# Another order of TensorE's and VectorE's work in the first small attention of a Perceiver block

## What is computed

```python
q = (layernorm(x) @ q_w.T + q_b)           # 16 heads of 32
k, v = ctx @ k_w.T + k_b, ctx @ v_w.T + v_b
q, k = apply_rope(q) * 32 ** -0.5, apply_rope(k)
scores = einsum('bhqd,bhkd->bhqk', q, k)   # only keys k <= q (a window of 64, 64 queries)
probs = softmax(scores)
x = x + einsum('bhqk,bhkd->bhqd', probs, v) @ o_w.T + o_b
```

## Time and profile before

| | us |
|---|---|
| median of 3 runs | 1521.74 |
| lowest and highest | 1520.28 and 1524.32 |
| the profiled execution | 1517.1 |
| its span, first to last instruction | 1515.1 |
| its mean granted TensorE clock | 0.963 |
| TensorE busy in the span | 1413.3 (93%) |
| VectorE busy | 727.6 (48%) |
| ScalarE busy | 509.7 (34%) |

### The profile page before, as it was taken

One profiled execution on the slowest core, in us unless ns is written; L12 is line 12 of the kernel. 1 busy time (PEld: TensorE's weight loads), 2 busy tenths in 40 slices (PEclk: granted clock), 3 DMA queues, 4 the chain that ended last, 5 costly groups with the idle time before them and its releaser, 6 DMA issues. The chain is left out here.

```text
span 1515.1 us, 26710 instructions
## 1 busy us (share of the span) xinstructions
PE 1413.3 (93%) x11200; PEld 1054.6 (70%) x11200; DVE 727.6 (48%) x1337; ACT 509.7 (34%) x839; POOL 368.6 (24%) x228
## 2 busy tenths in 40 slices
PE   7879988899989999999999999999999997997995
PEld 6747765455447788888787888888878865434783
DVE  6659769798463323323322233223232233676833
ACT  3414322333121153333432534334325343613702
POOL 7111000000140422222332313122313111306911
PEclk9799969999989999999999999999999999999997
DMA  5403100102024121111110211111102016003000
GB/s 204 167 1 132 42 35 1 77 0 84 0 91 143 57 63 33 52 38 57 37 55 30 64 33 52 38 57 39 55 28 64 23 51 256 1 0 132 0 1 28
DMA packets 49573, 88.01 MB, mean 58 GB/s; under 512 B 28584, under 2 KB 41136, under 8 KB 46128
## 3 DMA queue, kind: packets, MB, share of 16 engines
q1 hardware_dynamic: 49456, 86.32, 16.4%
HBM read 76.61 MB, written 9.70 MB: 57 GB/s over the span
## 5 line engine op out<-in xcount | busy, mean ns | idle before, releaser
L1338 POOL TENSOR_TENSOR ctx_hi<-ctx_raw,one 128x1536 fp32r<-128x1536 f32 (+1 forms) x32 | 91.5, 2860 | 567.3 <-DMA ctx_raw<-in_ctx 347.0
L1536 ACT COPY ET<-PS 128x512 f32<-128x512 f32 (+1 forms) x224 | 129.5, 585 | 277.0 <-PE PS L1440 201.6
L1639 DVE TENSOR_SCALAR_CACHE_REDUCE E<-PS 128x384 f32<-128x384 f32 (+1 forms) x256 | 131.8, 571 | 180.6 <-PE PS L1417 180.1
L1608 DVE TENSOR_TENSOR V<-PS,vbias 128x512 f32<-128x512 f32 (+1 forms) x104 | 71.8, 691 | 193.0 <-PE PS L1384 192.8
L1384 PE MATMUL PS<-ctx_raw_r,wk_hi 128*128 128x384 f32 (+1 forms) x512 | 128.2, 355 | 0.0
L1384 PE MATMUL PS<-wv_lo,ctx_hi 128*128 128x512 f32 (+1 forms) x416 | 127.6, 406 | 0.0
L1543 ACT ACTIVATE E<-E,peak 128x1601 f32<-128x1601 f32 x64 | 103.5, 1622 | 66.9 <-DVE peak L1644 66.9
L1440 PE MATMUL PS<-ident,E 128*128 128x128 f32 (+1 forms) x832 | 122.9, 273 | 0.0
L1384 PE MATMUL PS<-ctx_hi,wk_hi 128*128 128x384 f32 (+1 forms) x512 | 120.6, 357 | 1.5 <-POOL ctx_raw_r L1341 1.5
L1384 PE MATMUL PS<-wv_hi,ctx_hi 128*128 128x512 f32 (+1 forms) x416 | 120.4, 411 | 0.8 <-issue 0.8
L1341 POOL TENSOR_TENSOR ctx_raw_r<-ctx_raw,ctx_hi 128x1536 fp32r<-128x1536 f32 (+1 forms) x32 | 116.9, 3654 | 2.5
(11 more groups left out here) (320 smaller groups left out, 2217.0 us busy)
## 6 DMA issues: line engine op xcount, KB each, us to landing
ctx_raw<-in_ctx SPq DMA_DIRECT2D x24, 768.0 KB, 4.4
ctx_raw<-in_ctx_first SPq DMA_DIRECT2D x8, 900.0 KB, 4.5
rel_scr<-rel_out SPq DMA_DIRECT2D x8, 640.0 KB, 3.6
fwk<-in_fwk SPq DMA_DIRECT2D x1, 4096.0 KB, 12.2
fwv<-in_fwv SPq DMA_DIRECT2D x1, 4096.0 KB, 12.5
corr<-rel_scr SPq DMA_DIRECT2D x64, 48.0 KB
p_scr<-E SPq DMA_DIRECT2D x16, 192.0 KB, 2.3
near<-p_scr SPq DMA_DIRECT2D x64, 48.0 KB
```

Of the source, the lines that this page charges most:

```text
L1338: nc.gpsimd.tensor_tensor(ctx_hi[r][:, :, 0:n], ctx_raw[r][:, :, 0:n], one[:].unsqueeze(1).broadcast_to([P, KC, n]), ALU.mult).then_inc(S[ ...
L1536: nc.scalar.copy(ET[0:n, j % ET_RING, :], src[0:n, :]).then_inc(S["et_out"], 1)
L1608: v.tensor_tensor(V[0:rows, at % V_RING, :], bank(4 + NUMBER[unit] % 2)[0:rows, :], vbias[0:rows, :], ALU.add).then_inc(S["v_out"], 1)
L1639: v.tensor_scalar(E[:, p, k0:k0 + n], bank(r)[:, 0:n], 1.0, None, ALU.mult, ALU.max, accum_out=tops[:, p, c:c + 1]).then_inc(S["s_out"], 1)
```

## The change

In the call with the mask TensorE's list becomes S0 S1 V0 S2 C0 V1 S3 C1 V2 P0 C2 V3 P1 C3 P2 P3. On VectorE the residuals and moments of tiles 0 to 2 no longer stand between the softening and weighting of the tiles but behind the last weighting. The waits inside each step stay as they are. The call without the mask keeps its order.

```diff
             pe.wait_ge(s.loaded[w_out], 16)
-            scores(0)
-            for t in range(NT):
-                if t + 1 < NT:
-                    scores(t + 1)
-                if t >= 1:
-                    project(t - 1)
-                values(t)
-                context(t)
-            project(NT - 1)
+            if mask:
+                scores(0), scores(1), values(0), scores(2), context(0), values(1), scores(3), context(1)
+                values(2), project(0), context(2), values(3), project(1), context(3), project(2), project(3)
+            else:
+                scores(0)
+                for t in range(NT):
+                    if t + 1 < NT:
+                        scores(t + 1)
+                    if t >= 1:
+                        project(t - 1)
+                    values(t)
+                    context(t)
+                project(NT - 1)
...
                 other(2)
-                if t >= 1:
+                if t >= 1 and not mask:
                     residual(t - 1)
             if beside:
                 beside.finish(dve, ch)
+            if mask:
+                for t in range(NT - 1):
+                    residual(t)
```

## The result

The changed kernel takes 1510.94 us (median of 4 runs, 1510.06 to 1514.17), the kernel before 1523.03 in the same comparison (1520.28 to 1524.35): a ratio of 0.9926, 95% interval 0.9907 to 0.9944. That is 8.5 to 14.2 us less, a clear gain of 0.6 to 0.9%. The forecast was 1517.4, 4.3 us less, with 0.54 on no change and 0.42 on faster.

What follows compares the result with a forecast made beforehand. TensorE, with idle holes and a low clock, was taken to bound the first small attention. Reordering gains 3.40 us, taken as 4.3 for an earlier clock rise: 1521.7 - 4.3 = 1517.4 us, range 1511.5 to 1521.5.

Steps and rivals of the forecast that it cites:

- The holes ahead of C, P and C: First small attention, TensorE: idle times ahead of contexts and projections, 8.89 us in all, the first 3.80.
- the six waits: TensorE's idle times in the first small attention; no wait was to replace them from scores of tile 2 on.
- rival A: First small attention: clock back before tile 3's scores, VectorE becomes the bound; gain 8.2 us, 1513.5; chance 0.12.
- That reading of the transposes: Start of next stage: only transposes at 0.50 from 113.90 to 116.50, clock 1.00 from 117.40; transposes bring it back.
- The forecast case: First small attention: clock rises inside tile 0's projection, 3 us in, projection 5.0 us; gain 2.2 to 5.7, chance 0.62.
- The tail: Stage's end: residuals and three applies on VectorE ready just as tile 3's projection ends; costed at nothing.
- Rival B: First small attention: clock stays low through the run of projections; 10.2 us slower, 1531.9; chance 0.04.
- Rival C: Later stages: one clock fall more, gain 1.1, 1520.6, chance 0.13; one fewer, gain 7.5, 1514.2, chance 0.08.
- The base: Whole kernel: forecast starts from the runs' median 1521.74, 4.6 above the profiled execution's 1517.1.

Runs made afterwards that it cites:

- short kernels: Kernel before and changed kernel, each cut off behind the first small attention with the state stored there: 121.71 us before, 112.11 after.
- second trace of after: Changed kernel run again without an edit for another trace, against the kernel before: 1510.86 us in 6 runs, ratio 0.9924.
- short_after: Changed kernel cut off behind the first small attention, state stored there: 112.11 us (6 runs) against 121.71 for the kernel before cut alike.
- short_s3_first: Against short_after, the scores of tile 3 moved ahead of the context of tile 0 and weight transposes of tile 1: 119.22 us (4 runs).
- before_again: Kernel before, unedited, run again for a second trace: 1521.64 us (12 runs), ratio 1.0003; its time in the trace comparison is 1520.87.
- first trace of after: First profiled execution of the changed kernel, no further edit: 1511.36 us; the changed kernel's median was 1510.94.
- projections_late_only: Against the kernel before, projections and residuals late as in the change, scores still one tile ahead behind the context: 1521.8 us (12 runs), ratio 1.0003.
- short_before: Kernel before cut off behind the first small attention, state stored there: 121.71 us (6 runs, 120.33 to 123.43).
- short_filled_six: Against short_after, six useless matmul products added in TensorE's holes of the first attention: 112.77 us (4 runs) against 112.11.

## Why the prediction was right or wrong

**The direction and the mechanism** were right. The holes ahead of C, P and C were the gain, S2 moved into the first of them with its mask addition ready (the sum has 0.89 us to spare, not over 0.9; in the first trace it was 0.2, 66.84 to 67.08). From S3 on nothing replaced the six waits in the first trace; in the second, two of A's did, 1.11 and 0.91 us. That this stage can give nearly the whole gain is shown by the short kernels (9.6 of some 10 us).

**The size was too small by more than half**, through one step: where the clock comes back. The forecast put it under P0 and so charged S3, C1 and V2 at the low clock, 3.26, 0.55 and 0.93 us more than now. In the second trace of after and in short_after the clock is back ahead of S3: S3 takes 3.71 and 3.68 us, C1 0.99 and V2 1.09, and VectorE becomes the bound. That was rival A, with a chance of 0.12. In the short runs five of six are as fast as the trace with A's picture. The argument against A was the uninterrupted S2 at 0.50, and it stands for scores: short_s3_first shows 14 us of them that don't bring the clock back. But it was applied to the wrong stretch. Between S2 and S3 stand C0 and V1, and the prediction itself read, from the transposes of the next stage, that transposes bring the clock back; it used this for P0 behind V2 and not for S3 behind V1. In no trace of before does a V follow a C without a hole between them in the low stretch, so the rows bounded this case only from afar; in hindsight 0.12 was too little.

**That reading of the transposes** is right for the trace that it was made from and doesn't hold in the next ones. The same 16 transposes start the next stage in the other three traces of the whole kernels, and there the clock came back only at 121.0 (before_again), 114.9 (first trace of after) and 113.8 (second), each time under later matmuls. The first line below is the second trace of after over these transposes. A longer run of them does bear the reading out: the feed-forward layer starts with transposes alone, and in all four traces the clock comes back under them. The other two lines are the first trace of after, where they start at 265.39.

```profile
104.60:108.10 3.50, 3.50 (x16) 3.14 (x16) 2.74 (x5) 2.77 (x5) 3.50 (x1) 0.50 0.77 248
265.50:268.40 2.90, 2.90 (x14) 2.54 (x15) 2.69 (x7) 1.27 (x3) 0.00 (x0) 0.50 0.76 233
269.40:273.50 4.10, 3.92 (x26) 2.52 (x24) 2.44 (x4) 2.46 (x5) 0.00 (x0) 1.00 1.01 434
```

**A's own working** was right step for step. Its start times against the second trace of after: S3 76.68 and 76.19, V2 81.3 and 80.81, P0 82.3 and 81.74, C2 87.1 and 86.45, P1 89.9 and 89.28, P2 94.3 and 93.73. The constant 0.5 to 0.6 is a term of its own: the slot of V at the low clock was taken as 1.97 us from a V0 with nothing behind it; with S2 behind it the slot is 66.10 - 64.34 = 1.76, twice. So A gives 8.2 + 0.4, and 8.9 was measured.

**The forecast case** came in the first trace from S3 on only: P0 4.95 us against 5.0, rise 2.8 us in against 3. Ahead of S3 the clock was low from S0 on, back for S2 (67.08, 3.74 us) and fell once more before S3. The prediction had one fall and one rise, at the places of before.

**The tail** cost nothing, as worked out. The last apply of tile 2 ends at 103.37, when P3 (96.01 + 7.13 = 103.14) has just ended, and residual(3) follows at once (103.28); it starts 3.8 us behind P3's start (99.5), 3.81 before.

```profile
102.82 0.55 DVE L97 TENSOR_SCALAR XN<-X,mean_var,rstd 128x512 f32<-128x512 f32 x1 [0.46 <-POOL rstd L112]
103.28 0.68 DVE L420 TENSOR_TENSOR X<-PS,X 128x512 f32<-128x512 f32 x1
```

**Rival B** didn't come: from 87.8 to 103.0 the clock is 1.00. **Rival C**, a clock fall elsewhere, is seen between the two traces of before (6.1 us in the stretch that holds the second small attention) and possibly in projections_late_only. The two traces of after lie at the lower of these lengths (158.6 and 159.5 us, against 157.8 and 163.9); whether the changed kernel meets fewer falls there, two traces each can't say. **The base** of 1521.74 was right to use in place of the profiled 1517.1, which turned out the lucky end of 35 runs.

**The range** missed by 0.6 us. It was built as A less 2 us of scatter, 1511.5, as if A were the edge and not the middle. A's time with its own correction, 1521.74 - 8.6 = 1513.1, is still 2.2 us above the measured 1510.94; that rest is open, and falls of the clock elsewhere (rival C, or the one under P3 of short_before) are of this size.

## What to carry to other kernels

An order that closes TensorE's holes can gain twice, once for the holes and once for the clock that comes back earlier (in the first trace of after it gained by the holes alone, at the same mean clock). When a chance is put on the second, check each piece of work in the low stretch for what it does to the clock, not the longest piece alone. A rival whose working is sound and whose only obstacle is one unseen combination of rows deserves more than 0.12. One trace tells one meeting of the program with the clock; take a second before reading a rule from it. Once the softmax chain is the bound, a higher clock helps little (1.0 us up to V3 in short_filled_six), so find the next bound before paying for the clock. And a cut-down kernel that ends behind the changed stage measured in six runs what whole-program runs with several us of scatter elsewhere couldn't attribute.

## What the runs showed of the hardware

Scores (a 128x128 weight load for each 128x64 product, 32-bit) kept TensorE without a gap for 6.97 and 7.06 us with a hole of 1.48 between, and the granted clock stayed at 0.50 (1.2 GHz). Behind a context followed at once by transposes it was 1.00 (2.4 GHz) by 76.3 in the second trace of after and by 90.6 in short_s3_first, but not in the first trace of after, where it rose 2.8 us into the projection behind them. Transposes alone had it back in the feed-forward layer in all four traces of the whole kernels, and in one of these four behind the 16 transposes that start the stage after the first attention (1.00 from 117.4).

The same program met the fall and the rise at other places in other executions. In the first trace of after the clock fell under S0, was back by 67.2, behind S1 and V0, fell between 73.6 and 74.6 and was back at 87.6; in the second it fell under S1 and came back once, between 76.0 and 76.3. In short_after it fell under S0 as in the first trace, and S1 and V0 did not bring it back. In the three traces of before S1 and V0 have a hole of 3.80 us behind them and S2 is low.

The Trainium skill, "TensorE: Matmul & The Clock Gate", section "What's actually happening", has activity release the throttled clock. The traces agree in that each rise named here stands behind a stretch of work on TensorE; for S2, 6.9 us of scores without a gap at 0.50, they don't. Which work counts they don't settle.
